# A fused gated cross-attention and routed feed-forward kernel: softmax denominators in quarters of the tokens, in another order of steps

## The chip, the cores and the metric

The kernel runs on one core of one Trainium2 chip. The metric is device time in microseconds (us), start to end, of one execution. A profile of one execution goes with it: the start and duration of every instruction on TensorE (PE), VectorE (DVE), ScalarE (ACT) and GpSimd (POOL), and what SyncE (SP) gave to the DMA queues. PEld is TensorE's loading of weights, which the profile lists beside the products.

## What is computed

There are 8 batches of 512 tokens, each token a row of 512 numbers, and for each batch a context of 120 rows. Shortened:

```python
def reference(x, ctx, g_xattn, g_ffn, Wq, bq, Wk, bk, Wv, bv, We, be, Wo, bo, w_gate, w_expert, b_expert):
    q, c = layernorm(x), ctx
    Q, K, V = heads(q @ Wq.T + bq), heads(c @ Wk.T + bk), heads(c @ Wv.T + bv)   # 16 heads of 32
    attn = softmax(Q @ K.T / sqrt(32), axis=-1)
    out = merge(attn @ V)
    mixed = (mean over e of (out @ We[e].T + be[e])) @ Wo.T + bo
    x = x + tanh(g_xattn) * mixed
    hs = layernorm(x).reshape(-1, 512)
    probs = softmax(hs @ w_gate, axis=1)                  # 8 experts
    best = argmax(probs)                                  # one expert per token
    location = cumulative count of best, minus 1          # kept where location < 100
    ffn = gate * (dispatched rows @ w_expert + b_expert)  # zero for tokens beyond 100 per expert
    return x + tanh(g_ffn) * ffn
```

## The kernel before

**Tiling.** A batch is 512 tokens, held as four tiles of 128 tokens or as 512 columns. The 16 heads of 32 make four groups g of four heads; in a group the four heads j lie in four blocks of 32 partitions. A logit is held transposed: 120 context rows on the partitions, 512 tokens along the columns, four heads of a group in `probs` (fp32). The eight expert matrices are averaged once, and We and Wo are merged in the prologue into one matrix, `mixT`. Most fp16 products are done in three parts, high by high, high by low and low by high.

**The softmax.** `scores(b, g)` makes the logits of a group by four products of 97 rows and 512 columns, one a head, into four banks of PSUM (`quad`); `exp` on ACT turns them into `probs`, in two halves of two heads each. `values(b, g)` is two things: `weight_sums(b, g)`, which adds the rows of `probs` to denominators, and `value_sums(b, g)`, which multiplies `probs` by `v_all`. In the profile the first reads `den_sel` and the second `v_all`. Both use only 32 columns of the array, so four heads run in four column groups one beside the other. The maxima that are subtracted come from `max_scores(b, g)`, sixteen small products of 120 columns (`k_hi,q_hi`), and `maxima(b, g)` on DVE (`neg_max`).

**The denominators.** The denominators of a batch come together in one bank, `den_b`. Row (j, h, c, g) of its 128 partitions holds head j of group g, tokens of the half h, in 256 columns; `den_sel` has a selector of 32 columns for each of eight pairs (h, g) that sends the sum to the right rows, twice (c = 0 and c = 1). `reciprocal` on DVE takes all 256 columns; `rden_high` (ACT) and `rden_low` (DVE, `rden_both`) split the result into a high and a low fp16 part in the two copies. `spread_rden(b, g)` on PE then brings them to the 128 partitions of a group, by two products of 256 columns with `head_sel` (`rden_both,head_sel`), and `divide(b, g)` on DVE multiplies (`attn`). `spread_rden` of group 2 writes `den_b` again and group 3 `num_b`, so they wait for `divide` 0 and 1 (`s_at`).

**After the softmax.** `mix_high`, `mix_low`, `mix_begin` and `mix_middle` multiply by `mixT`, tile by tile of tokens; `x1_tile(b, t)` on DVE adds the result to x. `stats2` and `moments2` (`known`) take mean and variance of the new rows, `rstd2` on POOL (`veps`, `known`) the inverse root, `logit_scale` and `logit_gap` (`l_sub`, `l_max`, `l_dif`) the router's logits, `gate_exp` on ACT and `gate_value` on DVE the gate. `choose` picks the expert, `places` on PE and `read_places` (`place_all`, `place`) count, `enter_rows`, `enter_token` and `enter_places` (`word`, `entry`, `place_hot`) prepare a small product, `table_rows`, which writes the token lists; `add_table` reads it. In the last batch `expert_low` (`wqT_lo`) prepares a weight.

**The next batch's queries.** `stats1`, `moments1` (`mv`), `rstd1` on POOL (`rstd`, `std`), `normalise1` (`xn`), `x_hi` on ACT and `x_lo` on DVE (`xn_lo`) prepare the normalised rows of the batch after the next; SP transposes them by DMA into `xnT_hi` and `xnT_lo`. `route_x(b)` and `q_tile(b, g)` (`q_begin` and `q_end`, twelve products of 512 columns) read these, `q_high` (ACT) and `q_low` (DVE) take a tile of q out, `stack_q`, `shift_row` and DMAs put them into `q_stack`.

**What sets the order.** There is no scheduler. Each engine has a list of (step, batch ahead, argument), and `run(over, order)` issues the list once for each r in `over`, leaving out steps whose batch doesn't exist. So in the round r PE does the attention of batch r, the queries of batch r+1 and the router of batch r-1, while DVE normalises batch r+2. An engine does its list strictly in order, and semaphores (`s_...`) hold a step until its inputs are there. There are lists for r = -1 (beside the end of the prologue), for r = 0 to 5, for r = 6 and for r = 7.

## Time and profile before

| | us |
|---|---|
| median of 3 runs (lowest to highest) | 405.21 (405.14 to 405.38) |
| the execution that was profiled | 405.64 |
| its span, first to last instruction | 403.9 |
| PE busy | 396.3 (98%) |
| DVE busy | 333.3 (83%) |
| ACT busy | 225.3 (56%) |
| POOL busy | 167.4 (41%) |
| DMA moved | 63.19 MB |

Starts of `scores(b, 1)` (the first `q_stack,k_stack` after `table_rows`) are at 90.44, 126.62, 162.77, 198.72, 234.83, 270.79, 306.75 and 343.46 us of the span. These are the starts of the rounds r = 0 to 7, one every 36 us. The first 90 us are the prologue with the round r = -1, the last 60 the last batch with the experts' rows. TensorE's granted clock is full in all forty slices. PE's "busy" is modelled with overlapping instructions, so a time of one matmul (0.38 us for 512 columns) is longer than the distance from its start to the next one's start; the text below goes by distances.

### The profile page before, as it was taken

To read this page: it belongs to the slowest core of one execution; us is meant where nothing else is said; L and a number is where in the kernel's file an instruction comes from. 1 tells how busy PE (TensorE), PEld (TensorE's weight loads), DVE (VectorE), ACT (ScalarE), POOL (GpSimd) and SP (SyncE) were. 2 spreads that over 40 slices of the span, in tenths; PEclk is the share of its full clock that TensorE was granted. 3 is DMA by queue.
4 is the path that set the end of the run, shared out by engine and by line. 5 is a ranking of instruction groups with operands and counts; after the bars stand their busy time and mean duration, and the time that the engine had idled before them with its cause. 6 is when DMAs were issued, how large, how long until landed. Compare 5 with 4: busy or idle time off the path is not lost.

```text
span 403.9 us, 8706 instructions
## 1 busy us (share of the span) xinstructions
PE 396.3 (98%) x3102; PEld 182.2 (45%) x3102; DVE 333.3 (83%) x662; ACT 225.3 (56%) x320; POOL 167.4 (41%) x157
## 2 busy tenths in 40 slices
PE   7999999999999999999999999999999999899996
PEld 4556454443444444444444434444444444354444
DVE  6548456986898989998998998899897589779996
ACT  4436323568566754947485486748556474775110
POOL 2028999215080247309033530713271064460371
PEclk9999999999999999999999999999999999999999
DMA  8999991466059408823960692295169016241585
GB/s 278 334 389 394 344 390 41 91 124 165 2 111 199 174 1 170 217 98 85 175 223 1 142 238 104 60 183 189 54 133 242 5 33 175 84 132 28 99 172 180
DMA packets 65901, 63.19 MB, mean 156 GB/s; under 512 B 42277, under 2 KB 45617, under 8 KB 65859
## 3 DMA queue, kind: packets, MB, share of 16 engines
q1 hardware_dynamic: 60747, 56.19, 50.9%
q0 software_dynamic: 1632, 3.49, 3.1%
q10 hardware_dynamic: 3480, 2.96, 2.2%
q8 instruction: 26, 0.43, 0.4%
q14 instruction: 16, 0.13, 0.1%
HBM read 29.59 MB, written 12.98 MB: 105 GB/s over the span
## 4 chain that ended last, share of the span: by engine, by line
PE 71%; DVE 2%; issue 1%; ACT 1%; POOL 1%; DVEq 0%; ACTq 0%; POOLq 0%
PE ps L840 71%; ACT probs L1234 1%; PE ps L1161 0%; DVE xb L1567 0%; POOL known L1929 0%; POOL rstd L1929 0%; DVE bn_raw L1573 0%; ACT xn_hi L1234 0%; DVE xn L1500 0%; DVE base_cnt L1653 0%; DVE place_hot L1723 0%; POOL veps L1927 0%; ACT part_x L1234 0%; DVE xb L1865 0%; DVE wqT_lo L1678 0%
## 5 line engine op out<-in xcount | busy, mean ns | idle before, releaser
L1234 ACT ACTIVATE probs<-ps 120x1024 f32<-120x1024 f32 x64 | 62.0, 1024 | 19.4 <-PE ps L840 19.4
L1602 DVE TENSOR_REDUCE neg_max<-ps 128x16 bf16<-128x1920 f32 x32 | 68.7, 2148 | 3.7 <-PE ps L840 3.7
L1989 POOL TENSOR_TENSOR attn_lo<-attn,attn_hi 128x512 f16<-128x512 f32 x28 | 31.8, 1158 | 91.0 <-ACT attn_hi L1234 91.0
L840 PE MATMUL ps<-xnT_hi,wqT_hi 128*128 128x512 f16 x128 | 48.6, 380 | 0.0
L840 PE MATMUL ps<-mixT_hi,attn_hi 128*128 128x512 f16 x128 | 48.5, 379 | 0.0
L840 PE MATMUL ps<-mixT_lo,attn_hi 128*128 128x512 f16 x128 | 48.5, 379 | 0.0
L840 PE MATMUL ps<-xnT_lo,wqT_hi 128*128 128x512 f16 x128 | 48.5, 379 | 0.0
L1997 POOL TENSOR_TENSOR xb<-xb,mix_bias 128x512 f32<-128x512 f32 x32 | 39.6, 1271 | 15.4 <-DVE cb_col L1544 15.4
L1234 ACT ACTIVATE q_hi<-ps,bias_cols 128x512 f16<-128x512 f32 x32 | 22.1, 692 | 31.4 <-PE ps L840 31.4
L840 PE MATMUL ps<-q_stack,k_stack 97*128 97x512 f16 x128 | 33.9, 381 | 1.2 <-ACT probs L1234 1.0
L840 PE MATMUL ps<-probs,den_sel 120*32 120x256 f32 x512 | 34.1, 384 | 0.0
L840 PE MATMUL ps<-probs,v_all 120*32 120x512 f32 x256 | 33.5, 595 | 0.0
L840 PE MATMUL ps<-mixT_hi,attn_lo 128*128 128x512 f16 x128 | 33.0, 380 | 0.0
L840 PE MATMUL ps<-xnT_hi,wqT_lo 128*128 128x512 f16 x128 | 32.8, 379 | 0.0
L1234 ACT ACTIVATE q_stack<-q_hi 32x2048 f16<-32x2048 f16 x16 | 30.5, 1907 | 0.5
L1234 ACT ACTIVATE attn<-ps 128x512 f32<-128x512 f32 x32 | 19.0, 595 | 18.0 <-PE ps L840 18.0
L1595 DVE SCALAR_TENSOR_TENSOR q_lo<-ps,bias_cols,q_hi 128x512 f16<-128x512 f32 x32 | 23.8, 745 | 5.2 <-ACT q_hi L1234 5.0
L1561 DVE TENSOR_TENSOR attn<-ps,attn 128x512 f32<-128x512 f32 x32 | 20.6, 686 | 7.8 <-PE ps L840 7.5
L1234 ACT ACTIVATE attn_hi<-attn 128x512 f16<-128x512 f32 x32 | 19.7, 627 | 12.6 <-DVE attn L1561 12.6
L1567 DVE SCALAR_TENSOR_TENSOR xb<-ps,xb 128x512 f32<-128x512 f32 x32 | 21.8, 682 | 2.4 <-PE ps L840 2.1
L1927 POOL TENSOR_SCALAR veps<-mv 128x4 f32<-128x4 f32 x8 | 1.8, 230 | 49.5 <-DVE mv L1476 49.4
L840 PEld LDWEIGHTS ps<-probs,den_sel 120*32 120x32 f32 x512 | 14.1, 109 | 17.6 <-issue 11.2
(279 smaller groups left out, 792.7 us busy)
## 6 DMA issues: line engine op xcount, KB each, us to landing
xb<-in_x_dram SPq DMA_DIRECT2D x8, 1024.0 KB, 6.1
q_stack<-q_hi SPq DMA_DIRECT2D x48, 128.0 KB, 2.4
out_dram<-xb SPq DMA_DIRECT2D x6, 1024.0 KB, 7.4
raw<-in_L_xattn_We_dram SPq DMA_DIRECT2D x5, 1024.0 KB, 10.3
q_stack<-q_lo SPq DMA_DIRECT2D x32, 128.0 KB, 2.4
xb<-in_L_xattn_We_dram SPq DMA_DIRECT2D x3, 1024.0 KB, 10.3
k_stack<-k_scratch SPq DMA_DIRECT2D x8, 360.0 KB, 4.6
k_scratch<-k_hi ACTq DMA_DIRECT2D x16, 120.0 KB, 7.9
```

Of the source, the lines that this page charges most:

```text
L840: return e.matmul(out_, a, b, start=start, stop=stop, **kw)
L1234: return e.activation(out_, in_, func, **kw)
L1561: e.tensor_tensor(attn[:, g, :], (den_b, num_b)[g % 2], attn[:, g, :], ALU.mult).then_inc(s_at, 1)
L1567: e.scalar_tensor_tensor(out=row, in0=pair_b[t % 2], scalar=1.0 / (ATTN_SCALE * MIX_SCALE), in1=row, op0=ALU.mult, op1=ALU.add).then_inc(s ...
L1595: e.scalar_tensor_tensor(out=q_lo[:, g, :], in0=pair_b[g % 2], scalar=bias_cols[:, g:g + 1], in1=q_hi[:, g, :], op0=ALU.add, op1=ALU.subtr ...
L1602: e.tensor_reduce(maxed[:, :, :, g], quad[:, :, 0:NT * SK].rearrange("p j (t s) -> p t j s", t=NT), AX.X, ALU.max, negate=True).then_inc(s ...
L1927: e.tensor_scalar(tmp, mean_var, EPS, None, ALU.add).then_inc(s_ve, 1)
L1989: e.tensor_tensor(attn_lo[:, g, :], attn[:, g, :], attn_hi[:, g, :], ALU.subtract).then_inc(s_alo, 1)
L1997: ins = e.tensor_tensor(row, row, mix_bias[:, :], ALU.add)
```

## The change

**Quarters instead of halves.** `SQ` = 128 takes the place of `SH` = 256. A row of `den_b` is now (j, t, c, g) with t one of four quarters of the tokens, eight rows a quarter in each block of 32, and only 128 columns are in use. `weight_sums` makes four quarters by four heads, 16 products of 128 columns, where it made 8 of 256. `den_sel` becomes one array with two columns of ones, and each (t, g) takes a window of 32 columns of it. `head_sel` has four selectors a group, made by four DVE instructions in place of two; `spread_rden` is four products of 128 columns in place of two of 256. `rden`, `rden_hi` and `rden_both` have 128 columns, and with them `reciprocal`, `rden_high` and `rden_low`.

```diff
@@ -904,12 +907,12 @@
                             e.wait_ge(s_, n)
                     e.wait_ge(s_lraw, b)
                     e.wait_ge(s_sh, b + 1)
-                for h in range(2):
-                    sel = den_sel[:, (h * NK + g) * DK:(h * NK + g + 1) * DK]
+                for t in range(NT):
+                    first = SEL_AT - (2 * t * NK + g)
                     for j in range(HJ):
                         row = slice(j * DK, (j + 1) * DK)
-                        ins = mm(den_b[row, 0:SH], sel, probs[:, g % 2, j, h * SH:(h + 1) * SH],
-                                 start=(g == 0 and h == 0), stop=(g == NK - 1 and h == 1))
+                        ins = mm(den_b[row, 0:SQ], den_sel[:, first:first + DK], probs[:, g % 2, j, t * SQ:(t + 1) * SQ],
+                                 start=(g == 0 and t == 0), stop=(g == NK - 1 and t == NT - 1))
                 if g == NK - 1:
                     ins.then_inc(s_den, 1)
 
@@ -1043,8 +1046,9 @@
                     e.wait_ge(s_num, 4 * b + 4)
                 else:
                     e.wait_ge(s_at, 4 * b + g - 1)
-                mm(bank[:, 0:SH], head_sel[:, 0, g, :], rden_both[:, :])
-                mm(bank[:, SH:S], head_sel[:, 1, g, :], rden_both[:, :]).then_inc(s_bc, 1)
+                for t in range(NT):
+                    ins = mm(bank[:, t * SQ:(t + 1) * SQ], head_sel[:, t, g, :], rden_both[:, :])
+                ins.then_inc(s_bc, 1)
 
             def mix_steps(b, t, steps_of):
```

```diff
@@ -1548,7 +1535,7 @@
                 e.wait_ge(s_den, b + 1)
                 e.wait_ge(s_rhi, b)
                 e.wait_ge(s_rlo, b)
-                e.reciprocal(rden[:, :], den_b[:, 0:SH]).then_inc(s_rec, 1)
+                e.reciprocal(rden[:, :], den_b[:, 0:SQ]).then_inc(s_rec, 1)
 
             def rden_low(b, _):
                 e.wait_ge(s_rhi, b + 1)
```

**One wait more.** In the list of PE the first late unit of the prologue waits for the first `route_x_out`, which in the new order comes later:

```diff
@@ -843,6 +844,8 @@
                 u = units[i]
                 for s_, n in u["free"]:
                     e.wait_ge(s_, n)
+                if i == N_FIRST:
+                    e.wait_ge(s_pxe, 1)
                 if u["done"] == made[("k", 0, 0)]:
                     warm(u["bank"], NT)
                     warm(u["bank"], NT)
```

**Another order of steps** in r = -1, r = 0 to 5 and r = 6 on PE, ACT and DVE. The list of the last batch (r = 7) is as it was. On POOL `clear_rows` goes from behind the round r = 1 to its beginning, with all else as before. Of the lists of r = 0 to 5 for PE and DVE, two pieces:

```diff
             run(range(0, B - 2), [
...
-                (logits, -1, 0), (table_rows, -2, 0), (scores, 0, 1), (values, 0, 0), (scores, 0, 2),
-                (values, 0, 1), (route_x, 1, 0), (scores, 0, 3), (q_begin, 1, 0), (gate_mix, 0, 0),
...
+                (logits, -1, 0), (table_rows, -2, 0), (scores, 0, 1), (values, 0, 0), (values, 0, 1),
+                (route_x, 1, 0), (scores, 0, 2), (places, -1, 0), (q_begin, 1, 0), (gate_mix, 0, 0),
...
```

```diff
             run(range(0, B - 2), [
...
-                (reciprocal, 0, 0), (maxima, 1, 0), (rden_low, 0, 0), (q_low, 1, 1),
-                (divide, 0, 0), (divide, 0, 1), (divide, 0, 2), (divide, 0, 3), (q_low, 1, 2), (maxima, 1, 1),
...
+                (rden_low, 0, 0), (x_lo, 2, 1), (q_low, 1, 1), (divide, 0, 0), (divide, 0, 1), (divide, 0, 2),
+                (q_low, 1, 2), (divide, 0, 3), (x_lo, 2, 2), (maxima, 1, 1), (q_low, 1, 3), (maxima, 1, 2),
...
+                (x_lo, 2, 3), (x1_tile, 0, 3),
...
```

Of the four `x_lo` that DVE did in a row of steps ahead of the reciprocal, 0 now stands ahead of it, 1 behind `rden_low`, 2 behind `divide` 3, and 3 at the end of the list, directly ahead of `x1_tile` 3. SP transposes `xn_lo` when all four are done. ACT does `x_hi` 3 behind `q_high` 3.

In the list of PE for r = -1 `route_x` goes from ahead of `q_tile` 2 to behind `max_scores` 1. On DVE, r = -1, `scale_bias` goes to the beginning, and `normalise1` stands partly ahead of the late units. ACT follows: `route_x_out` ahead of `exp` 2, and the four `x_hi` spread through the list. In r = 6 DVE does `reciprocal` ahead of `q_low` 0, and `expert_low` at the very end; PE does the four `spread_rden` between the parts of `q_tile` 2.

The first place that the prediction speaks of is on PE at the start of the round r = 1. `q_stack,k_stack` is `scores` 1, 2 and 3, `den_sel` and `v_all` are `values`, `route_both` and `route_hi` are `route_x`. Before:

```order
L840 MATMUL ps<-q_stack,k_stack 128x512 x4
L840 MATMUL ps<-probs,den_sel 32x256 x8
L840 MATMUL ps<-probs,v_all 32x512 x4
L840 MATMUL ps<-q_stack,k_stack 128x512 x4
L840 MATMUL ps<-probs,den_sel 32x256 x8
L840 MATMUL ps<-probs,v_all 32x512 x4
L840 MATMUL ps<-xnT_hi,route_both 32x512 x4
L840 MATMUL ps<-xnT_lo,route_hi 32x512 x4
L840 MATMUL ps<-q_stack,k_stack 128x512 x4
```
After:

```order
L841 MATMUL ps<-q_stack,k_stack 128x512 x4
L841 MATMUL ps<-probs,den_sel 32x128 x16
L841 MATMUL ps<-probs,v_all 32x512 x4
L841 MATMUL ps<-probs,den_sel 32x128 x16
L841 MATMUL ps<-probs,v_all 32x512 x4
L841 MATMUL ps<-xnT_hi,route_both 32x512 x4
L841 MATMUL ps<-xnT_lo,route_hi 32x512 x4
L841 MATMUL ps<-q_stack,k_stack 128x512 x4
```
`scores` 2 now stands behind `values` 0, `values` 1 and `route_x`, where it stood between `values` 0 and 1.

The second is on PE in the same round, around `max_scores` 1 (`k_hi,q_hi`), with `rden_both,head_sel` for two `spread_rden` at a time, and `wqT` for the parts of `q_tile` 2. Before:

```order
L840 MATMUL ps<-rden_both,head_sel 128x256 x4
L840 MATMUL ps<-xnT_hi,wqT_hi 128x512
L840 MATMUL ps<-xnT_lo,wqT_hi 128x512
L840 MATMUL ps<-xnT_hi,wqT_lo 128x512 x4
L840 MATMUL ps<-k_hi,q_hi 128x120 x16
L840 MATMUL ps<-rden_both,head_sel 128x256 x4
```
After:

```order
L841 MATMUL ps<-rden_both,head_sel 128x128 x8
L841 MATMUL ps<-xnT_hi,wqT_hi 128x512
L841 MATMUL ps<-xnT_lo,wqT_hi 128x512
L841 MATMUL ps<-xnT_hi,wqT_lo 128x512 x4
L841 MATMUL ps<-rden_both,head_sel 128x128 x8
L841 MATMUL ps<-k_hi,q_hi 128x120 x16
```
The `spread_rden` of groups 2 and 3 now stand ahead of `max_scores` 1, where they stood behind it.

The third is on DVE, from `moments1` of batch r+2 (`mv`, r = 1 and 2) to `read_places` (`place_all`, `place`). Before:

```order
L1476 BN_AGGR mv<-bn_raw 128x2 x4
L1729 TENSOR_TENSOR table<-ps,table 100x64
L1573 BN_STATS bn_raw<-xb 128x6 x2
L1584 BN_AGGR known<-bn_raw 128x2 x4
L1500 TENSOR_SCALAR xn<-xb,mv,rstd 128x512 x4
L1637 TENSOR_REDUCE l_max<-l_raw 128x4
L1638 TENSOR_TENSOR l_dif<-l_raw,l_max 128x32
L1646 SCALAR_TENSOR_TENSOR ranked<-l_dif,rank8 128x32
L1649 TENSOR_REDUCE top_rank<-ranked 128x4
L1650 TENSOR_TENSOR choice<-ranked,top_rank 128x32
L1653 TENSOR_TENSOR base_cnt<-base_cnt,choice 128x8 x4
L1642 TENSOR_TENSOR l_sub<-l_dif,known 128x32
```
After:

```order
L1463 BN_AGGR mv<-bn_raw 128x2 x4
L1487 TENSOR_SCALAR xn<-xb,mv,rstd 128x512
L1571 BN_AGGR known<-bn_raw 128x2 x4
L1629 TENSOR_TENSOR l_sub<-l_dif,known 128x32
L1672 TENSOR_TENSOR place_all<-ps,choice 128x32
L1674 TENSOR_REDUCE place<-place_all 128x4
L1487 TENSOR_SCALAR xn<-xb,mv,rstd 128x512 x2
L1582 SCALAR_TENSOR_TENSOR q_lo<-ps,bias_cols,q_hi 128x512
L1487 TENSOR_SCALAR xn<-xb,mv,rstd 128x512
L1649 TENSOR_REDUCE l_sum<-l_exp 128x4
L1650 RECIPROCAL known<-l_sum 128x4
L1493 TENSOR_TENSOR xn_lo<-xn,xn_hi 128x4x128
```
`add_table`, `stats2`, `logit_gap` and `choose` now stand ahead of `mv`, and behind it follow `normalise1` 0, `moments2` (`known`) and `logit_scale` (`l_sub`), where the four `normalise1` and `choose` stood in between; `x_lo` 0 is alone ahead of the reciprocal.

The fourth is on DVE at the end of r = 6, with `wqT_lo` for `expert_low`, `table` for `add_table`, `xb` for `x1_tile` 3, `known` for `moments2`. Before:

```order
L1678 SCALAR_TENSOR_TENSOR wqT_lo<-xb,wqT_hi 128x1024
L1729 TENSOR_TENSOR table<-ps,table 100x64
L1567 SCALAR_TENSOR_TENSOR xb<-ps,xb 128x512
L1685 TENSOR_TENSOR place_all<-ps,choice 128x32
L1687 TENSOR_REDUCE place<-place_all 128x4
L1695 TENSOR_SCALAR word<-tile_iota 128x4
L1691 TENSOR_TENSOR entry<-choice,word 128x4x16
L1723 TENSOR_TENSOR place_hot<-place_iota,place 128x400
L1573 BN_STATS bn_raw<-xb 128x6
L1584 BN_AGGR known<-bn_raw 128x2 x4
```
After:

```order
L1672 TENSOR_TENSOR place_all<-ps,choice 128x32
L1674 TENSOR_REDUCE place<-place_all 128x4
L1682 TENSOR_SCALAR word<-tile_iota 128x4
L1678 TENSOR_TENSOR entry<-choice,word 128x4x16
L1554 SCALAR_TENSOR_TENSOR xb<-ps,xb 128x512
L1710 TENSOR_TENSOR place_hot<-place_iota,place 128x400
L1716 TENSOR_TENSOR table<-ps,table 100x64
L1560 BN_STATS bn_raw<-xb 128x6
L1571 BN_AGGR known<-bn_raw 128x2 x4
L1665 SCALAR_TENSOR_TENSOR wqT_lo<-xb,wqT_hi 128x1024
```
`expert_low` now stands behind `moments2`, and `read_places` and `enter_token` stand ahead of `x1_tile` 3.

## Rows read from the trace of the kernel before

**Rows 1.** The page, its first part (busy time, share, instructions of each engine).

```profile
PE 396.3 (98%) x3102; PEld 182.2 (45%) x3102; DVE 333.3 (83%) x662; ACT 225.3 (56%) x320; POOL 167.4 (41%) x157
```

**Rows 2.** Timeline of PE, batch 2: start, duration, engine, line, operation, out<-in, count.

```profile
164.69 1.04 PE L840 MATMUL ps<-probs,v_all 120*32 120x512 f32 x8
165.67 1.04 PE L840 MATMUL ps<-q_stack,k_stack 97*128 97x512 f16 x4
166.63 1.07 PE L840 MATMUL ps<-probs,den_sel 120*32 120x256 f32 x16
167.52 1.04 PE L840 MATMUL ps<-probs,v_all 120*32 120x512 f32 x8
168.38 0.40 PE L840 MATMUL ps<-xnT_hi,route_both 128*32 128x512 f16 x4
...
182.22 0.39 PE L840 MATMUL ps<-k_hi,q_hi 32*128 32x120 f16 x16
...
182.98 0.38 PE L840 MATMUL ps<-xnT_hi,wqT_hi 128*128 128x512 f16 x1
...
190.41 0.39 PE L840 MATMUL ps<-k_hi,q_hi 32*128 32x120 f16 x16
...
198.72 0.38 PE L840 MATMUL ps<-q_stack,k_stack 97*128 97x512 f16 x1
```

**Rows 3.** Timeline of PE in the prologue: fp32 products of 128 columns.

```profile
39.95 1.91 PE L405 MATMUL ps<-ident,xb 128*128 128x128 f32 x16
```

**Rows 4.** Timeline of DVE, batch 2; in brackets the idle time before and what ended it.

```profile
165.88 0.36 DVE L1476 BATCH_NORM_AGGREGATE mv<-bn_raw 128x2 f32<-128x6 f32 x4
...
167.74 1.89 DVE L1500 TENSOR_SCALAR xn<-xb,mv,rstd 128x512 f32<-128x512 f32 x4
...
171.44 1.89 DVE L1506 TENSOR_TENSOR xn_lo<-xn,xn_hi 128x512 f16<-128x512 f32 x3
...
175.39 1.76 DVE L1551 RECIPROCAL rden<-ps 128x256 f32<-128x256 f32 x1 [0.36 <-PE ps L840]
...
179.07 0.47 DVE L1556 SCALAR_TENSOR_TENSOR rden_both<-rden,low_row,rden_hi 128x256 f16<-128x256 f32 x1
180.02 0.75 DVE L1595 SCALAR_TENSOR_TENSOR q_lo<-ps,bias_cols,q_hi 128x512 f16<-128x512 f32 x1 [0.47 <-ACT q_hi L1234]
180.81 1.29 DVE L1561 TENSOR_TENSOR attn<-ps,attn 128x512 f32<-128x512 f32 x2
...
190.85 2.17 DVE L1602 TENSOR_REDUCE neg_max<-ps 128x16 bf16<-128x1920 f32 x1 [0.26 <-PE ps L840]
...
198.53 0.69 DVE L1567 SCALAR_TENSOR_TENSOR xb<-ps,xb 128x512 f32<-128x512 f32 x1
```

**Rows 5.** Timeline of POOL in the same batch.

```profile
168.96 1.12 POOL L1929 TENSOR_TENSOR known<-veps,neg_half 128x4 f32<-128x4 f32 x1
```

**Rows 6.** xnT_hi by tile, issue of its DMA to landing (min/median/max).

```profile
DMA to landing us min/median/max: 4.5/4.5/4.5
```

**Rows 7.** xnT_lo by tile, the same.

```profile
DMA to landing us min/median/max: 4.8/4.8/5.7
```

**Rows 8.** Timeline of PE in the prologue and in batch 0.

```profile
80.72 0.38 PE L588 MATMUL ps<-woT_hi,sum_hi 128*128 128x512 f16 x1 [0.27 <-issue]
...
98.49 0.38 PE L840 MATMUL ps<-xnT_lo,wqT_hi 128*128 128x512 f16 x1
99.02 0.18 PE L840 MATMUL ps<-gate_sum,part_hi 128*128 128x8 f16 x1
```

**Rows 9.** Timeline of DVE at the start of the last batch.

```profile
345.09 0.18 DVE L1685 TENSOR_TENSOR place_all<-ps,choice 128x32 f32<-128x32 f32 x1
...
345.88 0.57 DVE L1723 TENSOR_TENSOR place_hot<-place_iota,place 128x400 f16<-128x400 f32 x1
```

**Rows 10.** Timeline of PE, a little later.

```profile
350.31 0.61 PE L840 MATMUL ps<-q_stack,k_stack 97*128 97x512 f16 x2 [0.69 <-ACT probs L1234]
351.22 0.61 PE L840 MATMUL ps<-q_stack,k_stack 97*128 97x512 f16 x2 [0.31 <-ACT probs L1234]
```

169 lines of the change are left out of this document (84 added, 85 removed).

## The prediction

> **What bounds the kernel now.** I read the page first, then PE's timeline of one steady round (batch 2, the distance from one `scores` 1 to the next), then DVE's and POOL's beside it, and last the few places where PE stood still. PE is busy 98% of the span [rows 1], and a round is 35.95 us on it: 162.77, where the table of the starts has it, to 198.72 [rows 2]. So a microsecond counts if it is taken from PE's list, or from a wait of PE. DVE is at 83% over the span, but in a steady round it stands still for about 2.5 of the 36 us, and it has to be read as a second bound. Two of these waits are in brackets, 0.36 and 0.47 us [rows 4].
>
> **The tiling by itself.** On PE the same columns pass. An fp32 product goes as two passes, so a `weight_sums` is 16 passes of 256 columns before, in four rounds of four column groups, and takes 167.52 - 166.63 = 0.89 us [rows 2], 0.22 a round. Of 128 columns it is 32 passes, eight rounds. A lone fp32 pass of 128 columns, with its weights loaded for each, takes 1.91 / 16 = 0.12 at most [rows 3], about half of 0.22. So I take 8 x 0.11 = 0.88, no change, at most 8 x 0.12 = 0.96; with four `weight_sums` a round that is 0 to +0.3, and I take +0.05. `spread_rden` is four products of half the columns for two: 0. The sixteen `k_hi,q_hi` have 120 columns and load weights for each too: 0.76 us together with two `spread_rden` of 0.22 each [rows 2], so short products with a load each do run at their columns' rate. The two more `head_sel` instructions on DVE are in the set-up, where PE waits for DMA: 0. The reciprocal is what gains. It takes 1.76 us for 256 columns [rows 4], of which some 0.18 is fixed, as in DVE's smallest instructions; half of the rest is 0.79 off DVE. The bounds are 0 (a cost of the instruction, not of the column) and 0.88. `rden_low` gives half of its 0.47, 0.22.
>
> For the reciprocal the row gives (1.76 - 0.18) / 256 = 6.2 ns a column. The Trainium skill, "VectorE: DVE Perf Modes", the walkthrough of the 8-slice pipeline, says that it is an iterative divide with a repeat count of 8; at the 0.96 GHz of that page's specifications this would be an estimated 8.3 ns a column, 2.1 us before and 1.07 after, a saving of 1.07. The row is lower than that by its rate, and the sum goes by the row.
>
> **The order on PE.** A change between full-array and 32-column products costs time. From `v_all` to `scores` it is 165.67 - 164.69 = 0.98, from `v_all` to `route_x`, which has 32 columns too, only 168.38 - 167.52 = 0.86; from `scores` to `den_sel` it is 166.63 - 165.67 = 0.96, where four products of 512 columns take 0.86 otherwise [rows 2]. In the new order `scores` 2 no longer stands between `values` 0 and 1: one pair of changes less, 0.12 + 0.10 = 0.22. With +0.05 of the tiling, PE alone would do a round in 35.95 - 0.22 + 0.05, about 35.80.
>
> **What comes late next: DVE and POOL (r = 1 to 5).** `spread_rden` 3 waits for `divide` 1, and now stands ahead of `max_scores` 1, 0.42 us earlier in PE's list. I follow the loop that starts with `maxima` 3. Before, from its start (190.85, a round earlier 154.90) to that of `divide` 1 (180.81 + 0.60 = 181.41) pass 26.5 us [rows 4]. About 1.35 of them are idle: the 0.36 and 0.47, and half a microsecond of small gaps; 25.15 are work. After, work falls by 0.79 (reciprocal), 0.22 (`rden_low`) and 0.60 (one `x_lo` of the four, 1.89 / 3 less overlap, now stands behind the divides): 23.55. But two waits for POOL come open. `mv` is done at 166.24, and `normalise1` starts at 167.74; 1.50 us, in which DVE did other work before, and nothing after. POOL's second result, `known`, ends at 168.96 + 1.12 = 170.08 [rows 5], 3.84 after `mv`, and `logit_scale`, which had it for free behind `choose`, now comes after one `normalise1` (0.45) and four aggregates (0.28): another 3.84 + 0.05 - 1.50 - 0.73 = 1.66. Behind this wait are queued `read_places`, the other `normalise1`, `q_low`, and so the reciprocal and the divides. Together 23.55 + 1.50 + 1.66 = 26.7 to `divide` 1, 27.45 to its end. Then PE: `spread_rden` 3 0.22, `max_scores` 1 with its change of array 0.42, 182.98 to 190.41 = 7.43, and 0.44 from `max_scores` 3 to its maximum [rows 2, 4]: 8.5. The loop is 35.95 to 36.15 (as few or as many of the small gaps go), I take 36.05: +0.10 a round, with PE standing at `spread_rden` 3 for some 0.25. So the gain of 0.17 on PE's list is lost. It is four rounds of +0.10 (r = 2 to 5), and 0 for r = 1, which comes from a round without the router's steps: **+0.40**.
>
> **The transposes.** `x_lo` 3 now stands directly ahead of `x1_tile` 3, so it is done when that starts, at 198.53, 0.2 us ahead of `scores` 1 at 198.72 [rows 2, 4]; the transposing DMA of `xnT_lo` can go no earlier. `route_x` wants it behind `scores` 1, `values` 0 and `values` 1: 0.96 + 2 x 0.89 + 2 x 0.86 = 4.46 us after `scores` 1. If it lands 4.5 after its issue, as `xnT_hi` does [rows 6], it is in time by some 0.1 us; at the 4.8 of `xnT_lo` [rows 7], where two transposes went one behind the other, it is 0.2 late. A delay of up to 0.25 costs nothing, since PE would then only wait less at `spread_rden` 3. I take 0. The bounds are 0 and, with 5.7 [rows 7], 1.1 each.
>
> **The edges.** Round -1: the 0.27 of idle in front of the unit that reads `sum_hi` [rows 8] should go, since DVE does two `sum_low` ahead of `maxima` 2, and a change of array goes with `route_x` moved: **-0.37**. Round 0: no router's steps on DVE, so the 0.17 of PE's list stay; and before the gate products PE takes 99.02 - 98.49 = 0.53 [rows 8] where 0.22 are work, since ACT's `route_x_out` comes late; it is now ahead of `exp` 2: -0.17 - 0.25 = **-0.42**. Round 6: the switch is saved, but `spread_rden` 0 stands earlier, close behind `rden_low`, whose loop still has the wait for POOL: between -0.17 and +0.3, **+0.06**. Round 7: PE waits twice for `exp` 2, 0.69 and 0.31 [rows 10]. The chain to it is `x1_tile` 3, `moments2`, POOL's `known`, `l_sub`, `gate_exp` and `exp` on ACT. Of it, `read_places` and `enter_token` (345.88 - 345.09 = 0.79 [rows 9]) now lie ahead of `x1_tile` 3, where PE isn't waiting; `expert_low`, 1.2 us, lies in DVE's wait for POOL, with about 0.1 showing. **-0.70**. `clear_rows` moves into a stretch in which POOL idles.
>
> **The sum** is -0.37 - 0.42 + 0.40 + 0.06 - 0.70 = -1.03 us. The profiled execution, 405.64, would be 404.6; it lay 0.43 above the median of the runs, so the median goes from 405.21 to **404.2**. A difference of 0.2%, 0.8 us, is about the least that a measurement of this kernel can tell from no change.
>
> **Rivals.**
> First, the loop through DVE and POOL is shorter than I count, by 0.3 us a round: enough small gaps close, or the second `rstd` comes sooner because POOL isn't kept. For it: my 1.35 of gaps is the softest number, and the loop stands only 0.15 above PE's list. Against it: the waits for POOL are in the rows. Then the saving of 0.17 stays in six rounds: -0.37 - 0.42 - 1.0 - 0.70 = -2.5, **402.8**.
> Second, the other side: `xnT_lo` is late. If each landing takes 5.7 us, PE stands at `route_x` for 1.1 us; 0.25 of it are free in r = 1 to 5: 5 x 0.85 + 1.1 = +5.3, **409.5**. It turns the change into a loss from 0.4 us late on, a landing of 5.2. For it: the margin is a tenth of a microsecond, and a late DMA has no slack anywhere. Against it: `xnT_hi`, alone in its queue, landed after 4.5 each time.
> Third, the reciprocal isn't proportional, or a step waits that I took as ready: a loop longer by 0.2 to 0.5 a round. With 0.3 it is +1.5, **405.7**; the bound, a reciprocal that saves nothing, is +4, 408.2.
> Fourth, the weight loads of the short passes aren't hidden, and a round of 128 columns costs the 0.22 of one of 256: 32 x 0.87 = +28, 432. Against it [rows 3].
> The Trainium skill, "TensorE: Matmul & The Clock Gate", Part 3, the mechanism, says that a load is pulled ahead of running products when its row group differs or it goes to the background buffer; here all four heads use all rows, so only the buffer would hide it. By that rule's stricter half the fourth case would hold; the `k_hi,q_hi`, which lie in different row groups, don't test it, [rows 3] does, for one column group.
>
> **How the numbers follow.** Forecast (404.2, its own range 403.5 to 405.0): 0.44. First rival 0.22, second 0.13, third 0.18, fourth 0.03. The forecast's range lies on both sides of 404.4, 0.2% under the median: 0.25 faster, 0.19 same. The third rival is same up to 0.4 us a round, 0.11, and slower beyond, 0.07. So faster 0.22 + 0.25 = 0.47; same 0.19 + 0.11 = 0.30; slower 0.13 + 0.07 + 0.03 = 0.23. The range is 402.5 to 407.5: it takes in the forecast, the first rival, nearly all of the third and the near part of the second.
>
> **What would show it.** The list of PE: `den_sel` rounds 0.11 apart; one pair of changes less. The loop: in r = 2 to 5 DVE idle for POOL twice, 1.5 and 1.7 us, and PE idle some 0.25 at `spread_rden` 3, released by DVE's `attn`; rounds of 36.05 us. If rounds are 35.8 and PE doesn't wait there, the first rival holds; idle at the `route_x` products, released by a DMA, is the second; a `rden` of more than 1.0 us is the third. In round 7 `l_sub` 0.7 earlier against `scores` 1, and `q_stack,k_stack` with no first wait. I am wrong if the time outside rounds 0 to 5 moves by less than half of 1 us.

## The result and the profile after

The changed kernel takes **417.67 us** (416.68 to 419.13, four runs), the kernel before 405.29 beside it (405.14 to 405.40): a ratio of 1.031 [1.029, 1.034]. Run again in a later session, as the last experiment, it took 413.12 (two runs) against 405.24: 1.019 [1.017, 1.021]. So the change costs 8 to 12 us. The forecast was 404.2, with a range up to 407.5: the sign and the size are wrong. The first part of the page of the changed kernel stands beside [rows 1]:

```profile
PE 399.3 (96%) x3678; PEld 196.5 (47%) x3678; DVE 332.6 (80%) x663; ACT 223.0 (54%) x320; POOL 170.6 (41%) x157
```

The span is 414.9 us for 403.9. PE's busy time is up by 3 us with 576 more products, and DVE's is down by 0.7. Neither explains 11 us; the rest are waits. PE's waits of the changed kernel, the engine and line, who ended them, us in total, times, the longest:

```profile
PE ps L841 <- issue: 5.0, 6, 1.2
PE ps L841 <- DVE neg_max L1589: 2.7, 6, 0.6
PE ps L841 <- ACT xnT_hi L1231: 1.9, 1, 1.9
...
PE ps L841 <- ACT probs L1231: 0.3, 1, 0.3
```

Of these only the two waits for `exp` 2 in the last batch were there before [rows 10]: `probs`, and 0.61 of the 5.0 under `issue`. Where the waits stand, by rounds (distance between the starts of `scores` 1, and from the last of them to the end):

| kernel | start of r = 0 | r0 | r1 | r2 | r3 | r4 | r5 | r6 | r7 to end |
|---|---|---|---|---|---|---|---|---|---|
| before | 90.4 | 36.18 | 36.15 | 35.95 | 36.11 | 35.96 | 35.96 | 36.71 | 60.4 |
| changed | 89.7 | 36.36 | 36.71 | 37.99 | 37.95 | 37.74 | 37.75 | 36.91 | 63.8 |
| changed, second session | 89.9 | 36.36 | 36.70 | 37.95 | 37.99 | 37.72 | 37.71 | 36.91 | 60.4 |

The rounds r = 2 to 5 give 7.4 of the 11.0 us, r = 0, 1 and 6 0.9, the start of the span -0.7, and the last part 3.4 in the first profile and nothing in the second. The lengths of the rounds are repeated to 0.05 us; the loss at the end isn't.

**A slow round.** PE's timeline of batch 2, to be read beside [rows 2]:

```profile
162.77 1.11 PE L841 MATMUL ps<-q_stack,k_stack 97*128 97x512 f16 x4
163.81 1.08 PE L841 MATMUL ps<-probs,den_sel 120*32 120x128 f32 x32
164.71 1.04 PE L841 MATMUL ps<-probs,v_all 120*32 120x512 f32 x8
165.57 1.06 PE L841 MATMUL ps<-probs,den_sel 120*32 120x128 f32 x32
166.47 1.06 PE L841 MATMUL ps<-probs,v_all 120*32 120x512 f32 x8
168.69 0.40 PE L841 MATMUL ps<-xnT_hi,route_both 128*32 128x512 f16 x4 [1.16 <-issue]
...
182.63 1.03 PE L841 MATMUL ps<-xnT_hi,wqT_lo 128*128 128x512 f16 x4
183.50 0.77 PE L841 MATMUL ps<-rden_both,head_sel 128*128 128x128 f16 x8
184.20 0.39 PE L841 MATMUL ps<-k_hi,q_hi 32*128 32x120 f16 x16
...
189.44 0.39 PE L841 MATMUL ps<-k_hi,q_hi 32*128 32x120 f16 x16 [0.42 <-DVE neg_max L1589]
```

Two waits in brackets, and one without: `route_x` starts 168.69 - 166.47 = 2.22 us after `v_all`, where 0.88 are work, 1.3 late; `max_scores` 2 is 0.48 late; and the pair of `spread_rden` at 183.50 takes 184.20 - 183.50 = 0.70 for eight products, with the small wait that was forecast in it (0.16 over the same pair without one). What is left of the 37.99 us is 35.97.

**The transpose.** What SP gave to the queues there, and the tile `xnT_lo` over the span, issue to landing (min/median/max):

```profile
162.64 1.79 SPq L721 DMA_TRANSPOSE xnT_lo<-xn_lo  x1
164.47 1.14 SPq L730 DMA_DIRECT2D k_stack<-k_scratch  x1
```

```profile
DMA to landing us min/median/max: 4.3/5.7/6.0
```

Issued at 162.64, 0.13 ahead of `scores` 1, and landing 6.0 later, at 168.6: that is what `route_x` waited for. Issue by issue, r = 0 to 6: 4.6, 4.4, **6.0, 5.9, 5.7, 5.7**, 4.3. The four long ones are the four long rounds, and in each of them `route_x` starts 0.1 us after the landing.

**DVE and POOL** in the same batch, to be read beside [rows 4]:

```profile
168.99 0.36 DVE L1463 BATCH_NORM_AGGREGATE mv<-bn_raw 128x2 f32<-128x6 f32 x4
170.82 0.55 DVE L1487 TENSOR_SCALAR xn<-xb,mv,rstd 128x512 f32<-128x512 f32 x1 [1.47 <-POOL rstd L1907]
171.28 0.38 DVE L1571 BATCH_NORM_AGGREGATE known<-bn_raw 128x2 f32<-128x6 f32 x4
173.14 0.19 DVE L1629 TENSOR_TENSOR l_sub<-l_dif,known 128x32 f32<-128x32 f32 x1 [1.48 <-POOL known L1907]
...
178.07 0.95 DVE L1538 RECIPROCAL rden<-ps 128x128 f32<-128x128 f32 x1
...
181.20 0.69 DVE L1493 TENSOR_TENSOR xn_lo<-xn,xn_hi 128x512 f16<-128x512 f32 x1
...
185.78 1.43 DVE L1493 TENSOR_TENSOR xn_lo<-xn,xn_hi 128x512 f16<-128x512 f32 x1
187.14 2.15 DVE L1589 TENSOR_REDUCE neg_max<-ps 128x16 bf16<-128x1920 f32 x1
```

```profile
185.50 3.84 POOL L1967 TENSOR_TENSOR attn_lo<-attn,attn_hi 128x512 f16<-128x512 f32 x3 [0.46 <-ACT attn_hi L1231]
```

The two waits for POOL and the reciprocal came as forecast. But the same `xn_lo` takes 0.69 us alone and 1.43 where it stands beside POOL's `attn_lo`, and `maxima` 1 behind it is later by that. `max_scores` 2 waits for the bank that `maxima` 1 reads.

### The profile page after: what moved, and what is told of

Its sections match the earlier page's. It is cut to its first block, busy times and chain, and to the rows that moved or that the text cites. A ratio compares the mean times of both kernels' runs of the same rounds, so it can differ in the third digit from the quotient of the medians.

```text
span 414.9 us, 9859 instructions
## 1 busy us (share of the span) xinstructions
PE 399.3 (96%) x3678; PEld 196.5 (47%) x3678; DVE 332.6 (80%) x663; ACT 223.0 (54%) x320; POOL 170.6 (41%) x157
## 4 chain that ended last, share of the span: by engine, by line
PE 84%; DVE 9%; issue 3%; ACT 1%; DMA 1%; another core or an unknown queue 1%; POOL 1%; SPq 0%; DVEq 0%; ACTq 0%
PE ps L841 68%; PE ps L457 9%; DVE neg_max L1589 3%; PE ps L589 3%; PE ps L406 2%; DVE xn_lo L1493 2%; DVE attn L1548 2%; DMA raw<-in_L_xattn_Wk_dram 1%; ACT probs L1231 1%; DVE q_lo L1582 1%; DVE mixT_lo L399 1%; PE ps L1158 0%; POOL veps L1905 0%; POOL known L1907 0%
## 5 line engine op out<-in xcount | busy, mean ns | idle before, releaser
L1967 POOL TENSOR_TENSOR attn_lo<-attn,attn_hi 128x512 f16<-128x512 f32 x28 | 34.8, 1264 | 82.0 <-ACT attn_hi L1231 82.0
L841 PEld LDWEIGHTS ps<-probs,den_sel 120*32 120x32 f32 x1024 | 27.5, 110 | 16.3 <-issue 11.6
L841 PE MATMUL ps<-probs,den_sel 120*32 120x128 f32 x1024 | 34.9, 274 | 0.2 <-issue 0.2
L1231 ACT ACTIVATE attn_hi<-attn 128x512 f16<-128x512 f32 x32 | 18.8, 626 | 14.5 <-DVE attn L1548 14.5
L1493 DVE TENSOR_TENSOR xn_lo<-xn,xn_hi 128x512 f16<-128x512 f32 x28 | 23.4, 841 | 0.0
```

Source lines behind the costliest of these rows:

```text
L841: return e.matmul(out_, a, b, start=start, stop=stop, **kw)
L1231: return e.activation(out_, in_, func, **kw)
L1493: e.tensor_tensor(xn_lo[:, :, t, :], xn[:, t, :].rearrange("p (k s) -> p k s", k=NK), xn_hi[:, :, t, :], ALU.subtract).then_inc(s_xlo, 1)
L1967: e.tensor_tensor(attn_lo[:, g, :], attn[:, g, :], attn_hi[:, g, :], ALU.subtract).then_inc(s_alo, 1)
```

## The experiments

Their rounds in one table, read as above, with the medians and the ratio to the kernel before on the same chip (7, 11 and 12 are two runs each, the others four to eleven; "mended" is told under 6 and 9):

| kernel | median | ratio [95%] | r0 | r1 | r2 | r3 | r4 | r5 | r6 | to end |
|---|---|---|---|---|---|---|---|---|---|---|
| 1 quarters, old lists | 406.38 | 1.002 [1.001, 1.003] | 36.20 | 36.20 | 36.01 | 36.00 | 36.00 | 36.01 | 36.73 | 60.8 |
| 2 halves, new lists | 416.49 | 1.026 [1.024, 1.028] | 36.85 | 37.62 | 37.54 | 37.63 | 37.55 | 37.91 | 39.68 | 60.4 |
| 3 changed, `x_lo` 3 earlier | 412.46 | 1.017 [1.014, 1.019] | 36.43 | 36.82 | 36.70 | 36.70 | 36.70 | 36.90 | 36.80 | 63.1 |
| 4 new list on PE alone | 411.74 | 1.015 [1.014, 1.017] | 37.06 | 37.27 | 37.00 | 37.00 | 37.00 | 37.00 | 36.66 | 60.8 |
| 5 changed, `x_lo` 2 and 3 earlier | 409.84 | 1.011 [1.009, 1.012] | 36.38 | 36.94 | 36.84 | 36.81 | 36.82 | 37.05 | 36.80 | 60.4 |
| 6 as 4, ACT mended | 405.63 | 1.001 [1.000, 1.002] | 35.71 | 36.35 | 36.08 | 36.08 | 36.08 | 36.08 | 36.66 | 60.5 |
| 7 changed, shifted | 414.26 | 1.022 [1.017, 1.027] | 37.47 | 36.70 | 36.63 | 37.69 | 36.79 | 36.61 | 36.92 | 61.0 |
| 8 before, `expert_low` later | 404.39 | 0.997 [0.996, 0.998] | 36.17 | 36.15 | 35.96 | 35.96 | 35.96 | 35.95 | 36.83 | 59.7 |
| 9 halves, mended lists | 408.94 | 1.009 [1.008, 1.011] | 36.42 | 37.10 | 36.80 | 36.80 | 36.80 | 36.80 | 36.75 | 59.7 |
| 10 quarters, mended lists | 403.91 | 0.996 [0.994, 0.997] | 35.91 | 36.17 | 35.91 | 36.36 | 35.88 | 35.89 | 36.74 | 59.7 |
| 11 changed, old lists in r = 6 | 413.69 | 1.020 [1.018, 1.023] | 36.36 | 36.70 | 37.94 | 37.97 | 37.72 | 37.72 | 36.74 | 60.5 |
| 12 changed, again | 413.12 | 1.019 [1.017, 1.021] | 36.36 | 36.70 | 37.95 | 37.99 | 37.72 | 37.71 | 36.91 | 60.4 |

Two theories stood at the start. *The transpose*: rounds 2 to 5 are long because `x_lo` 3 gives `xnT_lo` to the queue too late. *The loop*: DVE's list with its two waits for POOL is the bound, and the transpose would find another wait if it came sooner.

### 1. The tiling alone

The changed kernel with the lists of before, on every engine, and without the added wait:

```diff
             run(range(0, B - 2), [
-                (logits, -1, 0), (table_rows, -2, 0), (scores, 0, 1), (values, 0, 0), (values, 0, 1),
-                (route_x, 1, 0), (scores, 0, 2), (places, -1, 0), (q_begin, 1, 0), (gate_mix, 0, 0),
+                (logits, -1, 0), (table_rows, -2, 0), (scores, 0, 1), (values, 0, 0), (scores, 0, 2),
+                (values, 0, 1), (route_x, 1, 0), (scores, 0, 3), (q_begin, 1, 0), (gate_mix, 0, 0),
```

> Quarters instead of halves, all lists of steps as before the change. Theory 1 (the loss comes from the order, above all from the late xnT_lo): the rounds stay at 35.9 to 36.0 us, the reciprocal takes 0.95 us, and the time is within 0.8 us of before, 404.8 to 405.9. Rival (the short fp32 passes, twice as many instructions on PE, cost time, in the rounds or in the last batch): rounds longer than 36.1, or the last batch 2 to 3 us longer, 407.5 or more.

Measured: +0.2%, and rounds of 36.00 for 35.96. The tiling costs PE 0.04 us a round (forecast 0.05) and, with the old lists, nobody wants the 0.8 us that it frees on DVE.

### 2. The order alone

The kernel before, with two halves, under the new lists and the added wait:

```diff
+                if i == N_FIRST:
+                    e.wait_ge(s_pxe, 1)
...
-                (logits, -1, 0), (table_rows, -2, 0), (scores, 0, 1), (values, 0, 0), (scores, 0, 2),
-                (values, 0, 1), (route_x, 1, 0), (scores, 0, 3), (q_begin, 1, 0), (gate_mix, 0, 0),
+                (logits, -1, 0), (table_rows, -2, 0), (scores, 0, 1), (values, 0, 0), (values, 0, 1),
+                (route_x, 1, 0), (scores, 0, 2), (places, -1, 0), (q_begin, 1, 0), (gate_mix, 0, 0),
```

> The new lists of steps, denominators in halves as before the change. Theory 1: PE still waits 0.9 to 1.2 us at route_x in the rounds 2 to 5, and with the reciprocal back at 1.76 us the wait for neg_max in front of max_scores 2 grows from 0.4 to about 1.2: 417 to 421. Rival (the tiling is at fault): no more than 409. The gap of 2 to 3 us in the last batch, if it comes from twice as many instructions on PE, is gone here.

Measured: +2.6%: the loss is in the order. Its waits on PE, and the landings:

```profile
PE ps L840 <- issue: 4.9, 8, 1.3
PE ps L840 <- DVE neg_max L1590: 2.5, 6, 0.4
PE ps L840 <- DVE attn L1549: 1.3, 6, 0.2
```

```profile
DMA to landing us min/median/max: 4.2/4.3/6.1
```

Here is the first surprise. With halves the transposes of r = 2 to 5 land after 4.25 to 4.31, and `route_x` doesn't wait; yet the rounds are 37.55. By distances PE loses 0.55 us at `spread_rden` 0 (an `issue` wait, behind a reciprocal of 1.76 us), 0.17 and 0.38 at `spread_rden` 2 and 3 (DVE's `attn`), and 0.48 at `max_scores` 2; without these the round of batch 2 is 35.96. So both theories hold, each for another kernel: the new order has more than one tight place, and which of them shows depends on the rest. In r = 6, the longest round of the table, the transpose did land after 6.1 us, and `route_x` was 1.5 late there; another 1.2 went ahead of the first `spread_rden`.

### 3. The transpose earlier

```diff
-                (x1_tile, 0, 0), (maxima, 1, 3), (route_sum, 0, 0), (x1_tile, 0, 1), (enter_rows, -1, 0),
+                (x1_tile, 0, 0), (maxima, 1, 3), (route_sum, 0, 0), (x_lo, 2, 3), (x1_tile, 0, 1), (enter_rows, -1, 0),
...
-                (x_lo, 2, 3), (x1_tile, 0, 3),
+                (x1_tile, 0, 3),
```

> The changed kernel with one step moved: x_lo 3 goes from directly ahead of x1_tile 3 to ahead of x1_tile 1, so that SP can transpose xn_lo right behind xn_hi. Theory 1: the waits of 0.9 to 1.2 us at route_x in rounds 2 to 5 are gone, about 4 us, 412 to 414; the wait for neg_max ahead of max_scores 2 stays (0.4 us), and the last batch is as it was. Rival (DVE's loop alone sets the rounds, and the wait at route_x only takes up its slack): the rounds stay at 37.5 us or more, with a longer wait for neg_max or at spread_rden, 416 to 418.

Measured: rounds of 36.70 for 37.74 to 37.99. PE around `route_x`:

```profile
167.71 1.07 PE L841 MATMUL ps<-probs,v_all 120*32 120x512 f32 x8
168.59 0.40 PE L841 MATMUL ps<-xnT_hi,route_both 128*32 128x512 f16 x4
```

0.88 from `v_all`, no wait. `xnT_lo` was the largest cause, 1.0 to 1.3 us in each of four rounds. A wait for `neg_max` remains (2.6 us in six, the longest 0.6).

### 4 and 6. The new list on PE, and all else as before

Quarters, PE's list of r = 0 to 5 as in the change but with `places` behind `q_end`, DVE's and POOL's lists as before, and on ACT a list to go with it (`route_x_out` ahead of `exp` 2, `x_hi` a little earlier). PE's list against the changed kernel's:

```diff
-                (route_x, 1, 0), (scores, 0, 2), (places, -1, 0), (q_begin, 1, 0), (gate_mix, 0, 0),
-                (scores, 0, 3), (q_end, 1, 0), (values, 0, 2), (values, 0, 3), (max_scores, 1, 0), (q_tile, 1, 1),
+                (route_x, 1, 0), (scores, 0, 2), (q_begin, 1, 0), (gate_mix, 0, 0),
+                (scores, 0, 3), (q_end, 1, 0), (places, -1, 0), (values, 0, 2), (values, 0, 3), (max_scores, 1, 0), (q_tile, 1, 1),
```

> Quarters; for the rounds 0 to 5 the new list of PE with places moved back to behind q_end, an ACT list that goes with it and has the four x_hi early, and DVE's list as before the change; rounds -1 and 6 as before. If the change of array is what the order on PE saves (0.22 a round) and the waits of the changed kernel all come from where DVE does x_lo, moments2 and logit_scale: rounds of 35.75 to 35.85 us, 403.7 to 404.4. If something else in PE's own list costs time (spread_rden ahead of max_scores 1, exp 2 behind route_x_out): rounds of 36 or more, 405 to 407.

Measured: 411.74, a miss of my own making. The waits name it:

```profile
PE ps L841 <- ACT attn L1235: 4.6, 6, 0.8
```

ACT did `x_hi` 2, `q_high` 0 and `x_hi` 3 ahead of `value_out` 2, so `values` 3 found its bank taken. Mended in ACT's list, with two `x_lo` on DVE behind `q_low` 0:

```diff
-                (x_hi, 2, 1), (exp, 0, 3), (gate_mix_high, 0, 0), (x_hi, 2, 2), (q_high, 1, 0), (x_hi, 2, 3),
-                (value_out, 0, 2), (value_out, 0, 3), (gate_exp, -1, 0),
+                (x_hi, 2, 1), (exp, 0, 3), (gate_mix_high, 0, 0), (q_high, 1, 0), (value_out, 0, 2), (x_hi, 2, 2),
+                (x_hi, 2, 3), (value_out, 0, 3), (gate_exp, -1, 0),
```

> The kernel with the new PE list, quarters and DVE's old list, in which value_sums 3 waited 0.76 us for ACT's value_out 2, since x_hi 2 and 3 stood ahead of it. Here value_out 2 stands ahead of them, and DVE's x_lo 2 and 3 behind q_low 0. If that wait was all: rounds of 35.8 to 36.1 us for 37.0, 405.0 to 406.5. The change of array then saves 0.2 a round on PE, and the quarters take 0.05 of it. Rival: ACT, with three exp, three x_hi and part_x in one stretch, is late elsewhere, and the rounds stay above 36.3.

Measured: 405.63, no difference from before. The wait for `attn` is gone and one stays at the start of the round:

```profile
197.51 0.17 PE L841 MATMUL ps<-gate_sum,part_lo 128*128 128x16 f16 x1
197.82 0.37 PE L841 MATMUL ps<-entry,place_hot 128*100 128x64 f16 x4
```

0.31 between two products that stand 0.03 apart otherwise: 0.28 for `place_hot` on DVE. Without it the round would be 36.08 - 0.28 = 35.80, which is what the forecast gave for PE alone. That is a subtraction, not a measurement: in experiment 10, where the wait is gone, most rounds are 35.88 to 35.91, since the first `scores` then takes 1.04 us for 0.96. So there is a saving on PE's list if `places` isn't put between two full-array steps of another shape, but what was measured of it is less than 0.1 us a round.

### 5. The two last x_lo behind route_sum

```diff
-                (q_low, 1, 2), (divide, 0, 3), (x_lo, 2, 2), (maxima, 1, 1), (q_low, 1, 3), (maxima, 1, 2),
-                (x1_tile, 0, 0), (maxima, 1, 3), (route_sum, 0, 0), (x1_tile, 0, 1), (enter_rows, -1, 0),
+                (q_low, 1, 2), (divide, 0, 3), (maxima, 1, 1), (q_low, 1, 3), (maxima, 1, 2),
+                (x1_tile, 0, 0), (maxima, 1, 3), (route_sum, 0, 0), (x_lo, 2, 2), (x_lo, 2, 3), (x1_tile, 0, 1), (enter_rows, -1, 0),
```

> Like the changed kernel with x_lo 3 early, and x_lo 2 moved too: from ahead of maxima 1, where POOL's attn_lo runs beside it and it took 1.43 us, to ahead of x_lo 3, behind maxima 3. Theory (DVE and POOL hold each other up when both read and write only SBUF): both x_lo take 0.6 to 0.7 us there, POOL's three attn_lo 3.4 again, neg_max 1 starts 1.4 earlier, the wait of 0.58 ahead of max_scores 2 is gone, rounds of 36.1 to 36.2 us for 36.70, about 3.2 us less than that kernel, 409.3. Rival (x_lo 2 was long because of a late xn_hi from ACT): it takes the same 1.4 us wherever it stands, or the wait ahead of max_scores 2 stays.

Measured: the wait for `neg_max` is gone, and so is the contention. `xn_lo` on DVE, durations min/median/max in ns, of the changed kernel and of this one:

```profile
L1493 DVE TENSOR_TENSOR xn_lo<-xn,xn_hi x28: 676/684/1432, 85.9 to 313.4; 128x512 f16<-128x512 f32 x28
```

```profile
L1493 DVE TENSOR_TENSOR xn_lo<-xn,xn_hi x28: 674/682/685, 86.4 to 305.9; 128x512 f16<-128x512 f32 x28
```

But the rounds are 36.8, by a third wait:

```profile
PE ps L841 <- DVE xb L1554: 3.0, 6, 0.5
```

Two `x_lo` of 0.6 us now keep `x1_tile` 1 from the bank that `mix_high` 3 wants. Of 0.5 us taken away 0.6 came back: in the new order DVE has no place for two `x_lo` behind the divides that PE doesn't feel.

### 7. The same kernel, its instructions shifted

`xnT_lo` was always issued at the same place, and it landed after 4.3 in some rounds and 5.7 to 6.0 in others. One more thing uses the DMA engines there. A line of the page's third part (queue and kind: packets, MB, share), of before and of the changed kernel:

```profile
q8 instruction: 26, 0.43, 0.4%
```

```profile
q8 instruction: 30, 0.49, 0.5%
```

Loads of instructions, 16 KB each; with 1,152 more instructions on PE (products and weight loads) there are four more of them, so they seem to be PE's. Most take about 1 us, and most landings of `xnT_lo` are long where one begins 1.7 to 4.5 us behind the issue. In the changed kernel these begin +4.0, +3.9, +3.3 and +3.3 us behind the four issues that land late, +4.3 behind that of r = 1 (landed after 4.4), and none in that stretch behind the one of r = 6 (4.3). To move them against the transposes and leave the steady rounds alone, 112 instructions of PE (56 short products and their weight loads) were put ahead of everything:

```diff
+            for _i in range(56):
+                warm(g1_b, 1)
```

> The changed kernel with 56 short warm-up products more at the very start of PE, 112 instructions, so that the same instruction lies elsewhere in the 16 KB pieces in which PE's instructions are fetched. Theory (in the last batch PE ran out of instructions: a fetch landed as it stood still, 1.3 to 2.7 us): the stall around weight_sums 3 of the last batch is gone or in another place, and from scores 1 of round 7 to the end it takes 60.6 to 61.5 us for 63.8. Rival (the order of round 6 delays something that the last batch needs): still 63 to 64 us, with the stall in the same place.

Measured, issue by issue:

| issue of r = | 0 | 1 | 2 | 3 | 4 | 5 | 6 |
|---|---|---|---|---|---|---|---|
| load of instructions begins, us behind the issue | +3.9 | +0.4 | 0.0 | +3.2 | none | +5.1 | +3.7 |
| landing, us | 6.2 | 5.2 | 4.3 | 5.7 | 4.3 | 4.3 | 4.3 |
| round, us | 37.47 | 36.70 | 36.63 | 37.69 | 36.79 | 36.61 | 36.92 |

```profile
DMA to landing us min/median/max: 4.3/4.3/6.2
```

The rounds r = 2, 4 and 5, 1 us too long in the changed kernel, are 36.6 to 36.8 here, and r = 0, which was short, is 37.5. The list of steps is the same; only the place in PE's stream is another. (In r = 1 the issue itself took 3.1 us for 1.8, behind another DMA.) So the length of a round follows the landing, some 1.1 us for 1.4 to 1.7 of landing, and the landing isn't a property of the round. That the instruction load is what delays it is likely but not shown. Over the 98 landings of `xnT_lo` in the fourteen profiles, 30 had a load of 16 KB begin in that stretch, and 22 of these were 5.6 us or more; of the other 68 two were, each with a load of 8 KB of another engine there. In five of the eight exceptions (r = 6 here and r = 1 of the changed kernel among them) the load itself took 2.0 to 3.0 us for about 1, so that in these the load may be what gave way. Experiment 2 fits too: no such load in r = 2 to 5 and landings of 4.3, one at +3.9 in r = 6 and 6.1; its r = 1 (+4.0, 4.6) doesn't. (The whole gained nothing: a `neg_max` wait of 2.1 us in the prologue came with the shift.)

### 8. expert_low later, in the kernel before

```diff
-                (stats2, 0, 2), (expert_low, 1, 0), (add_table, -1, 0), (x1_tile, 0, 3), (read_places, 0, 0), ...
+                (stats2, 0, 2), (add_table, -1, 0), (x1_tile, 0, 3), (read_places, 0, 0), ...
...
-                (enter_values, -1, 0), (add_values, -1, 0), (row_values, 0, 0), (expert_low, 0, 1),
+                (enter_values, -1, 0), (expert_low, 0, 0), (add_values, -1, 0), (row_values, 0, 0), (expert_low, 0, 1),
```

> The kernel before the change with one step moved: expert_low, 1.2 us on DVE, goes from ahead of x1_tile 3 of round 6 into round 7, behind enter_values, where DVE waited 1.2 us for PE. Theory (the gain forecast for round 7 is there if expert_low does not lie beside POOL's veps): known on POOL and l_sub 0.8 us earlier, PE's first wait for exp 2 (0.69) gone, 0.7 to 0.9 us less than before: 404.6 where before is at 405.4. Rival (another chain, x1_tile 3 behind mix_low 3, holds it): within 0.3 us of before.

Measured: 404.39, 1.0 us off, ratio 0.997 [0.996, 0.998]. POOL at the start of the last batch, first in the changed kernel, then here:

```profile
354.19 1.10 POOL L1905 TENSOR_SCALAR veps<-known 128x4 f32<-128x4 f32 x1 [8.64 <-DVE known L1571]
```

```profile
346.22 0.23 POOL L1927 TENSOR_SCALAR veps<-known 128x4 f32<-128x4 f32 x1 [9.31 <-DVE known L1584]
```

This instruction of four columns takes POOL 1.10 us beside DVE's `wqT_lo`, and 0.23 without it. In the kernel before it took 0.28, for `wqT_lo` was long done there. So the gain of this experiment comes from elsewhere: `x1_tile` 3 starts 0.29 us after `scores` 1 for 1.03, and `l_sub` 4.63 for 5.42. In the changed kernel itself `expert_low` was not moved.

### 9 and 10. Both tilings under the mended lists

The lists of 6, with the `expert_low` of 8 and `gate_value` behind `rden_low`, which brings `place_hot` forward:

```diff
-                (reciprocal, 0, 0), (maxima, 1, 0), (rden_low, 0, 0), (q_low, 1, 1),
+                (reciprocal, 0, 0), (maxima, 1, 0), (rden_low, 0, 0), (gate_value, -1, 0), (q_low, 1, 1),
```

> Halves, as before the change, with three moves: PE's list with scores 2 behind values 1 and route_x and the ACT list that goes with it, expert_low behind enter_values of the last batch, and gate_value on DVE from the end of the list to behind rden_low, where DVE was idle. Theory (0.22 a round from the changes of array, once table_rows needn't wait for place_hot; 0.9 in the last batch): rounds of 35.75 to 35.85 us for 35.96, 402.3 to 403.3, where before is at 405.4. Rival (with the reciprocal at 1.76 us DVE has no slack for a faster PE): rounds of 35.95 or more, no better than the kernel with expert_low alone moved, 404.4.

> The same three moves with quarters. Theory: DVE has 0.8 us a round more slack, PE pays 0.05 a round for the short passes: 0.3 to 0.5 us above the kernel with halves if that one isn't held by DVE, 402.8 to 403.8. Rival (DVE's slack matters): faster than the kernel with halves by 0.5 us or more.

Measured: 408.94 with halves, 403.91 with quarters. The same place in both, PE then DVE, halves first:

```profile
181.52 0.60 PE L840 MATMUL ps<-rden_both,head_sel 128*128 128x256 f16 x4 [0.58 <-issue]
```

```profile
177.28 1.75 DVE L1545 RECIPROCAL rden<-ps 128x256 f32<-128x256 f32 x1
```

```profile
179.92 0.61 PE L841 MATMUL ps<-rden_both,head_sel 128*128 128x128 f16 x8
```

```profile
176.42 0.95 DVE L1546 RECIPROCAL rden<-ps 128x128 f32<-128x128 f32 x1
```

With the new PE list the reciprocal is on the path, and quarters are worth 5.0 us; with the old list (experiment 1) they were worth less than nothing. Halves with the new list are 3.7 us slower than before. The kernel of experiment 10 has the lowest time of all, 0.4% under before. 0.3% of it is `expert_low` (experiment 8); the intervals of 8 and 10 overlap, so a gain of quarters and order beside it isn't shown.

### 11 and 12. The end of the span

In the first profile of the changed kernel PE stood still once more, in the last batch:

```profile
363.62 1.06 PE L841 MATMUL ps<-probs,v_all 120*32 120x512 f32 x8
366.62 0.38 PE L841 MATMUL ps<-wqT_hi,xnT_hi 128*128 128x512 f16 x1 [1.93 <-ACT xnT_hi L1231]
```

The trace has the step of the denominators' semaphore 2.3 us after the start of the last product of `den_sel`, where it is 0.3 in other rounds, and ACT and DVE waited for theirs. Two theories: the order (with the old lists of r = 6 it goes), or a chance of the execution (it goes in a repeat of the same kernel too). Experiment 11 is the changed kernel with the three lists of r = 6 as before:

```diff
             run([B - 2], [
-                (table_rows, -2, 0), (logits, -1, 0), (scores, 0, 1), (values, 0, 0), (values, 0, 1),
+                (logits, -1, 0), (table_rows, -2, 0), (scores, 0, 1), (values, 0, 0), (scores, 0, 2),
```

> The changed kernel with the three lists of round 6 as before the change. If the new order of round 6 causes the stall of 1.3 to 2.7 us around weight_sums 3 of the last batch: from scores 1 of round 7 to the end 60.4 to 60.8 us for 63.8. If the stall comes and goes with something outside the order (it was there in two kernels, small in three, absent in three): it may be there or not, and veps beside expert_low takes 0.3 us instead of 1.10.

and experiment 12 the changed kernel, unedited:

> The changed kernel unchanged, for a second look. If the lateness of xnT_lo is set by a fetch of PE's instructions at 3.2 to 4.0 us behind the issue, the fetches lie in the same places and the same rounds show landings of 5.7 to 6.0 us (rounds 2 to 5), the others 4.3 to 4.6. If the stall in the last batch is a matter of the order or of the place of the instructions, it is there again with 2 to 3 us; if it is chance, it is gone or of another size. 416.5 to 419.

Measured: neither has it, 60.5 and 60.4 us to the end. In 12 the same two places follow each other closely:

```profile
362.86 1.06 PE L841 MATMUL ps<-probs,v_all 120*32 120x512 f32 x8
363.85 0.39 PE L841 MATMUL ps<-wqT_hi,xnT_hi 128*128 128x512 f16 x1
```

So the 3.4 us are no fixed cost of the change's order: the same kernel runs without them. They are the distance between the two profiled executions, 416.68 and 413.38 us; of the other three executions of the first session, which were longer still, there is no trace. The same stall is in the profile of experiment 3, which took 63.1 us to the end with its semaphore step at 1.6, and a small one (0.5 to 0.8) in 1, 2 and 4; these four ran on one chip. In 5 to 12, on two other chips, the step is at its 0.3 or 0.4. Whether the chip, the session or the code makes it isn't separated, and what causes it stays open.

## Why the prediction was wrong

**The transposes: the step that failed.** "I take 0" stood on a margin of 0.1 us and on the landings of `xnT_hi`, 4.5 each time [rows 6]. The margin was right: issued at 162.64, wanted 4.7 later. The landing wasn't 4.5 but 4.3 to 4.6 or 5.7 to 6.0. [Rows 7] had the 5.7, as a maximum; I read it as the effect of a second transpose in the queue and gave the case 0.13. The second rival is what happened in r = 2 to 5, at its far end: 1.1 to 1.3 us late in each, 4.9 together. Nor were 0.25 us of a delay free: PE loses 0.16 at `spread_rden` 3 in the round of batch 2 with the late transpose and in the same round of experiment 7 with an early one. A median of seven landings says little where the slack is 0.1 and the loss is on one side only: the term should have been a mean over the rows seen, and one landing of 5.7 among seven already makes it 0.85 / 7 = +0.1 a round.

**x_lo behind the divides: a cost not seen.** The forecast moved `x_lo` 2 at its row's duration, 0.6. Beside POOL's `attn_lo` it took 1.43, `maxima` 1 came 0.75 later, and PE waited 0.42 to 0.58 at `max_scores` 2 in each of r = 0 to 5 (2.7 us). That is the second half of the third rival, "a step waits that I took as ready", at the 0.5 a round that it allowed; experiment 5, with `x_lo` 2 moved away, has it no more, and every `xn_lo` takes 0.67 to 0.69; at 0.69 in its old place it would have been 0.74 shorter, more than the 0.48 that PE lost in a steady round. The forecast followed the loop to `spread_rden` 3 and no further, and never asked what POOL was doing at the place to which a step was moved. The Trainium skill, "SBUF — State Buffer", "Who interferes with whom", says that a VectorE instruction with two SBUF inputs contends with a GpSimd instruction that reads SBUF, that the shared ports are an exclusive lock, and that the order of issue decides who is blocked. The rows agree: the first `attn_lo` ran from 185.50 to about 186.67, `xn_lo` started at 185.78 and ended at 187.21, 0.54 behind it, and the `attn_lo` after it took 1.61 us for 1.16. That rule spoke against this change and the forecast didn't weigh it.

**The tiling: right.** `den_sel` takes 0.90 for 32 passes (forecast 0.88, at most 0.96), the reciprocal 0.95 us (forecast 1.76 - 0.79 = 0.97), `rden_both` 0.34 for 0.47, 0.13 of the 0.22 expected. The fourth rival is out, and so is the first half of the third.

**The loop: right in its parts.** The waits for POOL measured 1.47 and 1.48 (forecast 1.50 and 1.66), and the wait at `spread_rden` 3 0.16 (forecast 0.25). A round of the changed kernel in which the transpose lands early is 36.6 to 36.8 (experiment 7), where 36.05 was forecast; 0.48 of the difference is `max_scores` 2. No round is 35.8, so the first rival is out.

**PE's list: over-counted.** 0.22 was to be saved by one pair of changes less, and is, between `values` 0 and 1. But `places`, which I didn't follow, now stands between `scores` 2 and the parts of `q_tile` and gives about 0.08 back, and from `q_end` straight to `den_sel` another 0.09: without its waits the round is 35.97, not 35.80. With `places` behind `q_end` it is 35.88 to 35.91 in most rounds of experiment 10.

**The edges.** r = -1: -0.75 and -0.56 in two profiles for -0.37; but with the same lists for it the start of r = 0 lay anywhere from 89.7 to 91.2 (experiments 3, 5, 11 and 12), so a term of that size can't be tested by it. r = 0: +0.18 for -0.42; the wait for `route_x_out` went, a `neg_max` wait of 0.58 came. r = 1: +0.55 for 0, the same wait. r = 6: +0.20 for +0.06. r = 7: 0.0 for -0.70. There the mechanism was right and its cover wrong: `expert_low` was to lie in DVE's wait for POOL "with about 0.1 showing", but it delayed the very instruction that DVE waited for, `veps`, by 0.8 us. `l_sub` came 356.46 - 351.12 = 5.34 us after `scores` 1, before 348.88 - 343.46 = 5.42. Experiment 8, which moves it behind `enter_values` in the kernel before, has a gain of that size, 1.0 us. By the prediction's own sign, that the time outside r = 0 to 5 moves by at least 0.5 us, it failed as well: the second profile has -0.56 + 0.20 + 0.0 = -0.4 there.

**The sum** of what was measured: -0.7 (r = -1), +0.9 (r = 0, 1, 6), +7.4 (r = 2 to 5: 4.9 the transposes, 1.9 `max_scores` 2, 0.6 `spread_rden` 3), 0 (r = 7), 7.6 to 7.9 us, and 3.4 more in the first profile by a stall that the same kernel also runs without. Two sums of the recorded text are off by a tenth: the first rival gives 405.21 - 2.5 = 402.7, and the second turns the change into a loss from a landing of 5.1 on. Neither bears on the result.

## What to carry to other kernels

A DMA that is issued so late that it makes its reader by a tenth of a microsecond is a loss, not a draw: take the longest landing seen, not the median. Before a step is moved on DVE, look at what POOL does at the new place, above all for operations of two inputs; "hidden in a wait for POOL" is wrong if the step slows POOL. The price of an edit depends on the list around it: the quarters, which make DVE's work shorter, gained nothing under the old lists and 5.0 us under the new PE list, which without them was a loss. Together they are level with the old kernel or a little better; a gain beyond that of `expert_low` isn't shown.

## What the runs showed of the hardware

- A transposing DMA of the same size, issued at the same place of a round with the same neighbours in its queue, lands after 4.3 to 4.6 or 5.7 to 6.2 us, and in which rounds it is late changed when PE's instruction stream was shifted by 112 instructions. Over all profiles 22 of 30 landings with a load of 16 KB of instructions beginning 1.7 to 4.5 us behind the issue were 5.6 us or more, and 2 of 68 others.
- A VectorE instruction of two SBUF inputs (`xn_lo`) that starts 0.3 us behind GpSimd's `attn_lo` takes 1.43 us for 0.69; a GpSimd instruction of four columns (`veps`) takes 1.10 for 0.23 behind DVE's `wqT_lo` of 1.2 us.
- A reciprocal on DVE takes 0.95 us for 128 columns and 1.75 to 1.76 for 256: 6.3 ns a column over a fixed 0.15.
- fp32 products of 128 columns in four column groups, a weight load for each, run at the rate of those with 256 columns: 0.90 us for 0.89.
